# Serving the first group of a CIN tower from the resident small tables, with the loads, VectorE's opening work, the picks and the last gram product in another order

## The reference

```python
e = jnp.stack([tbl_0[ids[:, 0]], ..., tbl_25[ids[:, 25]]], axis=1)      # [512, 26, 32]
x1 = einsum('bik,bjk,hij->bhk', e, e, W1) + b1[None, :, None]           # h = 128
x2 = einsum('bik,bjk,hij->bhk', x1, e, W2) + b2[None, :, None]
z = sum(concatenate([x1, x2], axis=1), axis=-1)                         # [512, 256]
h = concatenate([z, dense_ctx], axis=1)                                 # [512, 272]
h = maximum(h @ W_top1 + b_top1, 0); h = maximum(h @ W_top2 + b_top2, 0)
y = h @ W_top3
```

## Time and profile before

| | us |
|---|---|
| median of 3 runs (171.09, 173.31, 173.40) | 173.31 |
| the profiled execution | 174.04 |
| span of its instructions | 171.9 |
| TensorE busy | 147.7 (86%) |
| VectorE busy | 109.5 (64%) |
| GpSimd busy | 93.9 (55%) |
| ScalarE busy | 70.7 (41%) |

### The profile page before, as it was taken

One profiled execution on the slowest core, in us unless ns is written; L12 is line 12 of the kernel. 1 busy time (PEld: TensorE's weight loads), 2 busy tenths in 40 slices (PEclk: granted clock), 3 DMA queues, 4 the chain that ended last, 5 costly groups with the idle time before them and its releaser, 6 DMA issues.

```text
span 171.9 us, 3203 instructions
## 1 busy us (share of the span) xinstructions
PE 147.7 (86%) x1172; PEld 134.6 (78%) x1172; DVE 109.5 (64%) x423; ACT 70.7 (41%) x209; POOL 93.9 (55%) x100
## 2 busy tenths in 40 slices
PE   6609999506999999879998998999799889999695
PEld 6406666505999798869987997899699889999693
DVE  6779469999999699998055999703769990000000
ACT  2203888304268803134645202564540146780032
POOL 3778787777787777777777777777700000000000
PEclk9965999985599999999999999999999999999999
DMA  5994320100003120101030220003012000203000
GB/s 138 399 283 141 128 74 11 19 14 11 13 12 55 28 73 14 19 11 15 15 55 14 55 57 11 15 11 57 14 25 65 0 0 0 44 0 75 9 0 0
DMA packets 8535, 8.53 MB, mean 50 GB/s; under 512 B 3128, under 2 KB 7650, under 8 KB 8340
## 3 DMA queue, kind: packets, MB, share of 16 engines
q1 hardware_dynamic: 2668, 4.70, 8.2%
q10 hardware_dynamic: 2908, 2.12, 6.2%
q0 software_dynamic: 2944, 1.51, 5.4%
HBM read 7.28 MB, written 1.04 MB: 48 GB/s over the span
## 4 chain that ended last, share of the span: by engine, by line
PE 62%; DVE 14%; DMA 8%; POOL 8%; ACT 4%; issue 3%; DVEq 0%; SPq 0%
PE ring L599 28%; POOL emb L300 8%; PE z2p L638 7%; PE z2p L629 5%; PE z2p L634 5%; PE h2y L679 4%; DVE r L481 3%; DMA emb<-in_tbl,idx 3%; DMA gram<-gram_scratch 2%; DVE emb L460 2%; PE ring L622 2%; DVE l_a L489 2%; PE ring L613 2%; PE h1p L670 2%; DVE ctx_x L456 2%
## 5 line engine op out<-in xcount | busy, mean ns | idle before, releaser
L300 POOL DMA_INDIRECT emb<-in_tbl,idx x92 | 93.0, 1011 | 29.6 <-issue 27.7
L599 PE MATMUL ring<-r,l_a 128*106 128x104 f32 x256 | 27.8, 272 | 1.3 <-DVE r L481 1.3
L599 PEld LDWEIGHTS ring<-r,l_a 128*106 128x106 f32 x256 | 26.9, 187 | 2.4 <-issue 2.4
L599 PE MATMUL ring<-r,l_b 128*106 128x104 f32 x256 | 25.9, 258 | 2.2 <-DVE emb L460 2.2
L599 PEld LDWEIGHTS ring<-r,l_b 128*106 128x106 f32 x256 | 24.8, 173 | 3.0 <-DVE emb L460 2.9
L571 PE MATMUL ring<-w1s,w2t 128*128 128x352 f32 x52 | 17.6, 504 | 4.3 <-DVE w1s L353 4.3
L773 ACT COPY t_a<-ring 106x416 f32<-106x416 f32 x32 | 16.2, 506 | 12.1 <-PE ring L599 11.7
L571 PEld LDWEIGHTS ring<-w1s,w2t 128*128 128x128 f32 x52 | 10.9, 211 | 10.6 <-DVE w1s L353 4.4
L489 DVE TENSOR_TENSOR l_b<-sg_b,l_b 128x192 f32<-128x192 f32 (+5 forms) x72 | 15.5, 299 | 0.0
L489 DVE TENSOR_TENSOR l_a<-sg_a,l_a 128x192 f32<-128x192 f32 (+5 forms) x72 | 15.5, 299 | 0.0
L456 DVE TENSOR_TENSOR ctx_x<-ring,mask 128x512 f32<-128x512 f32 x6 | 4.2, 692 | 17.6 <-PE ring L613 17.3
(11 more groups left out here) (129 smaller groups left out, 181.4 us busy)
## 6 DMA issues: line engine op xcount, KB each, us to landing
w2t<-in_L_rec_W SPq DMA_DIRECT2D x1, 1664.0 KB, 7.3
emb<-in_tbl,idx POOLq DMA_INDIRECT x92, 2.4
wt<-in_W_top SPq DMA_DIRECT2D x2, 512.0 KB, 8.4
octet<-in_octet_ids SPq DMA_DIRECT2D x1, 750.0 KB
gram_scratch<-t_a ACTq DMA_DIRECT2D x4, 169.0 KB
gram<-gram_scratch ACTq DMA_DIRECT2D x4, 126.0 KB
small_tbl<-in_tbl SPq DMA_DIRECT2D x4, 125.0 KB
w<-in_L_rec_W SPq DMA_DIRECT2D x1, 338.0 KB, 7.8
```

Source lines behind the costliest of these rows:

```text
L300: pool.indirect_dma_start(out=emb[:, g, f * K:(f + 1) * K], out_offset=None, in_=a[f"tbl_{f}"][:, :], in_offset=bass.IndirectOffsetOnAxis( ...
L599: last = pe.matmul(ps[0:MC, i * 4 * NF:(i + 1) * 4 * NF], L[c][:, t, :], R[:, t, :, :].rearrange("p q f -> p (q f)"), start=True, stop=True)
```

## The change

The small tables now also serve group 0 (`OH_G` = 0): 88 gathers instead of 92, `octet` has 2048 columns instead of 1536, and there is a `look_up(0)` between the 13th and the 14th mix product and a `pick(0)` after `one_hot`. SP issues w1 ahead of w2t, and `octet`, `place_in` and the four tables ahead of the dense weights. R is zeroed at once, after the w1 sums, and `split_wt1c` moves behind `pick(1)`. In groups 1 and 2 the two look-ups stand behind blocks 9 and 11 instead of both behind block 9. In the last group `own` comes ahead of `gram_part`, and the tail takes the second half of z first, in banks that nobody else holds.

```diff
-OH_AT = NB + 1
+OH_AT = (NB + 1, NB + 3)
-OH_G = 1
+OH_G = 0
-        wt1c_rest = [sb(f"wt1c_rest{i}", [P, D1]) for i in range(2)]
+        wt1c_rest = [sb("wt1c_rest", [P, D1]), wt1c_in]
-        h1_tail = [bank[:, 0:P] for bank in ring + [sg[0]]]
...
-        turns = [("pre", n) for n in range(EARLY)] + [("t", n) for n in range(2 * NB)]
+        OH_FIRST = at[("mix", NH - 1, 1)] + 1
+        turns = [("pre", n) for n in range(OH_FIRST)] + picks(0) + [("pre", n) for n in range(OH_FIRST, EARLY)]
+        turns += [("t", n) for n in range(2 * NB)]
...
-                if n == OH_AT:
-                    turns += picks(g + 1)
+                if n in OH_AT and picks(g + 1):
+                    turns += [picks(g + 1)[OH_AT.index(n)]]
...
+        h1_tail = [bank[:, 0:P] for bank in ring if bank is not bank_of("z1", G - 1)] + [bank[:, 0:P] for bank in sg]
...
+            sp.dma_start(w1[:, :, :], a["L0_rec_W1"]).then_inc(w1_in, 16)
             sp.dma_start(w2t[:, :, :], a["L0_rec_W2"]).then_inc(w2_in, 16)
-            sp.dma_start(w1[:, :, :], a["L0_rec_W1"]).then_inc(w1_in, 16)
+            sp.dma_start(octet[0:OR, :, :], a["octet_ids"]).then_inc(octet_in, 16)
+            sp.dma_start(place_in[:, :, :], a["place_ids"]).then_inc(place_loaded, 16)
+            for i, f in enumerate(OH):
+                sp.dma_start(small_tbl[0:OR, i, :], a[f"tbl_{f}"].rearrange("(r a) d -> r (a d)", a=OCT)).then_inc(small_in, 16)
             sp.dma_start(wt1[:, :, :], a["W_top1"][0:2 * P, :].rearrange("(c p) n -> p c n", p=P)).then_inc(wt_in, 16)
...
-            dve.memset(R[:, 0:NT // 2, :, :], 0.0)
...
-            dve.memset(R[:, NT // 2:NT, :, :], 0.0).then_inc(zeroed, 1)
-            split_wt1c()
+            dve.memset(R[:, :, :, :], 0.0).then_inc(zeroed, 1)
             dve.wait_ge(zeroed, 1)
             one_hot()
+            pick(0)
             build_a(0)
...
             pick(1)
+            split_wt1c()
...
-            def look_up(g):
+            def look_up(g, ks=(0, 1)):
-                for kind, n in picks(g):
+                for kind, n in [p for p in picks(g) if p[1] % 2 in ks]:
...
+                own()
                 gram_part(g)
-                own()
-                pe.wait_ge(z1_ready, g + 1)
-                for m in range(M1):
-                    pe.matmul(h1_tail[m], wt1c[:, m * P:(m + 1) * P], ctx_t[:, g, :], start=True, stop=False)
-                    pe.matmul(h1_tail[m], wt1[:, 0, m * P:(m + 1) * P], z[:, 0, :], start=False, stop=False)
-                pe.wait_ge(z2_ready, g + 1)
+                pe.wait_ge(z2_ready, g + 1)
+                for m in range(M1):
+                    pe.matmul(h1_tail[m], wt1c[:, m * P:(m + 1) * P], ctx_t[:, g, :], start=True, stop=False)
+                    pe.matmul(h1_tail[m], wt1[:, 1, m * P:(m + 1) * P], z[:, 1, :], start=False, stop=False)
+                pe.wait_ge(z1_ready, g + 1)
...
-            for n in range(EARLY):
+            for n in range(OH_FIRST):
+                prepare(n)
+            look_up(0)
+            for n in range(OH_FIRST, EARLY):
                 prepare(n)
...
-                    if n == OH_AT:
-                        look_up(g + 1)
+                    if n in OH_AT:
+                        look_up(g + 1, (OH_AT.index(n),))
...
-            z_copy(G - 1, (0, 1))
+            z_copy(G - 1, (1, 0))
```

More of the change, by code:

```diff
@@ L272, in _ @@
             sp.dma_start(wt2[:, :, :], a["W_top2"].rearrange("(c p) n -> p c n", p=P)).then_inc(wt_in, 16)
[L273 to L276, removed]
             for g in range(G):
@@ L651, in z_group @@
                     return
+                own()
                 gram_part(g)
-                own()
+                pe.wait_ge(z2_ready, g + 1)
+                for m in range(M1):
+                    pe.matmul(h1_tail[m], wt1c[:, m * P:(m + 1) * P], ctx_t[:, g, :], start=True, stop=False)
+                    pe.matmul(h1_tail[m], wt1[:, 1, m * P:(m + 1) * P], z[:, 1, :], start=False, stop=False)
                 pe.wait_ge(z1_ready, g + 1)
                 for m in range(M1):
-                    pe.matmul(h1_tail[m], wt1c[:, m * P:(m + 1) * P], ctx_t[:, g, :], start=True, stop=False)
-                    pe.matmul(h1_tail[m], wt1[:, 0, m * P:(m + 1) * P], z[:, 0, :], start=False, stop=False)
-                pe.wait_ge(z2_ready, g + 1)
-                for m in range(M1):
-                    pe.matmul(h1_tail[m], wt1[:, 1, m * P:(m + 1) * P], z[:, 1, :],
+                    pe.matmul(h1_tail[m], wt1[:, 0, m * P:(m + 1) * P], z[:, 0, :],
                               start=False, stop=True).then_inc(h1_done, 1)
```

## The result

| | before | after |
|---|---|---|
| median of 20 runs (lowest to highest), us | 172.73 (171.09 to 173.70) | 174.76 (173.06 to 177.02) |
| ratio of the two, 95% interval | | 1.0113 [1.0078, 1.0148] |
| the profiled execution, us | 174.04 | 175.13 |
| its span, us | 171.9 | 173.3 |
| mean granted TensorE clock in it | 0.95 | 0.95 |

The changed kernel is 2.0 us slower; the forecast was 1.1 us faster. The clock line of the page after, against the earlier trace rows: the low stretch at group 0's blocks is still there, only later (slices 10 to 12), and a new one lies at the first look-up (slice 6).

The account below looks back on a forecast made before the run. TensorE was taken as the bound from 42.62 us on, before that group 0's gathers, then VectorE. Start, clock and split +1.0, picks -0.7, gram -1.4 gave -1.1: median 173.31 to 172.2 us, range 169.7 to 175.0.

Parts of the forecast that it names:

- The clock: At group 0's blocks: after a shorter TensorE idle time the clock stays at full speed, -2.45 us, otherwise 0.
- rival 1: The clock falls before group 0's blocks all the same: +0.7 us in all, 174.0 us, chance 0.28.
- The start: Group 0's part 0 on VectorE waits for tables, look-up and picks, starting at 27.0 instead of 25.19: +1.8 us.
- Behind the delay nothing new waits: Between part 0's later start and group 0's first block, no new wait was found; no size of its own.
- The split: Ahead of group 1's R copies, 3.2 us of work against 2.2 of room: first block 1.0 us later than before.
- Picks apart: In groups 1 and 2, TensorE's waits for picks shrink from 1.09 to 0.74 us a group: -0.7 us in all.
- Gram later: In the last group's tail, `own` fills TensorE's 1.43 us wait for gram, which goes: -1.4 us.
- The sum: Whole kernel: +1.0 at group 1's first block, -0.7 for picks, -1.4 for gram, together -1.1 us.
- What bounds the start: Before part 0, slow loads of `octet` and tables, 117 GB/s on few DMA engines: tables in at about 22.5 us.

Follow-up runs that it names:

- e2: The changed kernel with `split_wt1c` ahead of `pick(1)` instead of behind it: 174.29 us, ratio 1.0033 to the kernel before.
- e3: The changed kernel with `octet` and each small table loaded in two pieces, of 112 and 13 rows, instead of one of 125: 171.70 us, ratio 0.9854.
- e6: The changed kernel with both look-ups of groups 1 and 2 again behind block 9 and `gram_part` again ahead of `own`: 176.49 us, ratio 1.0269.
- e8: The changed kernel with `octet` and small tables loaded in pieces of 112 and 13 rows and `split_wt1c` ahead of `pick(1)`: 170.34 us, ratio 0.9882.
- e1: The kernel before with only the look-ups of groups 1 and 2 set two blocks apart and the new tail: 170.04 us, ratio 0.9854.
- e7: The kernel before with only the tail changed (`own` ahead of the gram product, second half of z first): 169.80 us, ratio 0.9862.
- e12: The changed kernel with idle TensorE products: 14 before the first look-up, 24 instead of 7 before the vh transposes, 10 behind them: 173.06 us, ratio 1.0022.
- e5: e8 with `look_up(0)` behind 8 mix products instead of 13: 168.29 us, ratio 0.9746 to the kernel before.
- e4: The changed kernel with idle TensorE products: 14 before `look_up(0)` and 24 instead of 7 before the va transposes: 174.38 us, ratio 1.0097.

## Why the prediction was wrong, point by point

- **The clock (-2.45): the step that failed.** "For the shorter one I take it as likelier that the clock stays." The idle time was as forecast (4.34 us, within 3.4 to 4.4), but the clock fell all the same and group 0's side a took 8.42 us. So it did in every profile with about that idle time: e2 (4.28 us idle, side a 8.02), e3 (4.33, 9.16), e6 (4.29, 7.94) and e8 (4.29, 7.70). With the longer idle time of the old start the clock fell as well, and the blocks ran at half in one profile of three (before, 8.62) and at full in two (e1 and e7, 6.19). What differed is when the clock rose again, from 41.0 us in e1 to 50.1 in the changed kernel. The prediction let the fall hang on the length of the idle time, though its own rows had a fall behind 4.30 us; no run bears that out. This was rival 1, whose sum is +0.7. Brought about by force for look-up and blocks (e12), the full clock gives back 0.9%, 1.6 us of the 3.1 between forecast and result.
- **The start (+1.8): right in its mechanism, too small.** `octet` was in at 17.14 (forecast 18.3) and the look-up began at 22.45 (22.5), 22.52 in e2 and 22.27 in e6. What was missed is that TensorE, idle for 3.50 us there, ran the look-up at half clock: the first pair took 1.76 us in place of the 0.95 in the sum. Part 0 came at 28.01, not 27.0; in e2 and e6, with the look-up at full clock, at 27.43 and 27.19. So it is +2.8 in this execution and +2.0 to +2.2 in those two. "Behind the delay nothing new waits" held: the 2.82 us are unchanged at the first block.
- **The split: right.** With the low clock the sum had R copies end at 81.45; they ended at 82.34, late by the start's 0.9 to 1.0. With the clock held (e12) TensorE waits 1.49 us for them where "about 1.5" was forecast. Moved ahead of pick(1) it leaves no wait in e2's profile, whose blocks run at half clock.
- **Picks apart (-0.7): right**, -0.65, with waits of 0.35 and 0.36 where 0.35 to 0.4 was forecast.
- **Gram later (-1.4): right**, -1.7: the wait of 1.43 us is gone. From the start of the last side-b sums to the first tail product it is 6.70 in place of 8.40 us; behind that both kernels take the same time.
- **The sum.** With +1.0 more at the start and 0 for the clock the forecast's terms give +1.7 for -1.1; the spans of the profiles have +1.4. The medians have +2.0. The sum was made against a profiled execution of before that was 0.75 us longer than the median of its like, and carrying its distance from the median over to the new kernel was the last, smaller error. It shows in e12 too: its profile is 1.1 us shorter than that of before (170.8 against 171.9), as much as was forecast, and its median is not.
- **What bounds the start: right**, and e3 shows it by its repair. By the rule of the Trainium skill (DMA: Bandwidth & Descriptors, "Why a DMA increments its semaphore by 16 and not by 1") a load of 112 rows gets 16 engines where one of 125 gets 5; the trace agrees, with 94.8% of the 16 engines' time in SP's queue between 10 and 12 us in place of 32.1%, and `octet` in at 14.21 us in place of 17.14. The prediction used that rule to accept the low rate; it could have read the repair from it.

Left open: what decides how long the low clock lasts, and so in which executions it reaches group 0's blocks; in how many of the timed executions it did, which a mean clock does not tell; and where the 0.75 us of the profiled execution of before lie.

## What to carry to other kernels

A source that replaces another (tables for gathers) brings its own loads, and its gain is the difference of the two arrival times plus the work behind the new one; here the gathers of part 0 were in by 20.2 us (SP, done with its loads then, passed the part on without a wait), but the tables, on few DMA engines, at 22.4 and the picks at 28. Before counting on a clock gain, look at several profiles and at when the clock rises in each, not only at whether it falls; and look for what idles ahead of each new product, since a wait that ends in half-speed work costs twice. Work that hides in one engine's wait must be moved into another wait, not in front of a chain that another engine waits for.

## What the runs showed of the hardware that was not expected

- SP was held 11.07 us in issuing the four tables behind `octet` (first row, the changed kernel); in e5, with both in pieces over all engines, eight pieces took 3.68:

```profile
3.06 11.07 SPq L276 DMA_DIRECT2D small_tbl<-in_tbl  x4
```
```profile
3.60 3.68 SPq L279 DMA_DIRECT2D small_tbl<-in_tbl  x8
```

- With the loads in two pieces (e3) SP's queue went from 32.1% to 94.8% of the DMA engines' time between 10 and 12 us, and from 0.27 to 0.49 MB. Between 14 and 16 us all DMA together went from 140 to 293 GB/s, though by then other loads of the list were moving.
- TensorE's clock fell to half (1.2 of 2.4 GHz) in or just behind every idle stretch of 4.3 to 5.8 us ahead of the transposes of vh, between 34.7 us (e7) and 39.8 us (the changed kernel), and stayed low for 3.4 us (e1) to 10.2 us (before, the changed kernel). It also fell behind idle times of 2.71 us (e4) and 3.50 us (the changed kernel's look-up), but not at the look-up of e2 after 2.57 and of e6 after 3.14.
